# State-space stage of a ViT layer: three table products handed to GpSimd, weight loads begun by ScalarE, a third store buffer, a last chunk with summed operands

## The reference

```python
P = dt_Lambda[..., None] * pos - P_max[..., None]      # token h (128), state n (64), position l (1024)
Wc = Wc * num * _reciprocal(den * Lam, EPS)            # Wc: x as complex numbers
K = jnp.einsum('chn,hnl->chl', Wc, jnp.exp(P))         # c: 64 batch rows
return K.real
...
h = _L0_tok_ref(...)                                   # this stage: h0, 64 x 128 x 1024
h = h + _L0_attn_ref(_layernorm(h), Wq, Wk, Wv, Wo)    # second stage of the kernel, not touched
h = h + _L0_ffn_ref(_layernorm(h), A, B, Wr, br)       # second stage, not touched
```

## Time and profile before

| | us |
|---|---|
| median of 3 runs (2502.73 to 2509.3) | 2504.96 |
| the profiled execution | 2504.22 |
| its span, first to last instruction | 2502.4 |
| first matmul of s4_stage | 42.06 |
| first instruction of layer_stage | 300.40 |

### The profile page before, as it was taken

The page is one execution under the profiler, slowest core; times in us unless marked ns, Lnnn a source line. Parts: engine busy times, 40 slices in busy tenths (PEclk is TensorE's granted clock), DMA queues, the critical chain, the costliest instruction groups (busy, mean ns, idle before and its releaser), DMA issues.

```text
span 2502.4 us, 58994 instructions
## 1 busy us (share of the span) xinstructions
PE 2349.1 (94%) x18752; PEld 1245.7 (50%) x18752; DVE 1952.3 (78%) x7939; ACT 1850.1 (74%) x6398; POOL 1629.6 (65%) x1508
## 2 busy tenths in 40 slices
PE   2888679999999999999999999999999999999986
PEld 2677534444455544454455454444555545444543
DVE  8888547888788778788787778788887778887864
ACT  5777547777777777777777777777777777777773
POOL 1233147777777777777777777777777777777772
PEclk9999889999999999999999999999999999999997
DMA  2777559999999999999999999999999999999984
GB/s 74 215 210 213 166 103 167 176 184 184 182 186 188 183 177 179 186 185 184 181 188 186 185 174 181 185 185 184 184 187 184 179 181 182 184 186 186 182 164 101
DMA packets 1199527, 443.66 MB, mean 177 GB/s; under 512 B 1149552, under 2 KB 1151856, under 8 KB 1199216
## 3 DMA queue, kind: packets, MB, share of 16 engines
q1 hardware_dynamic: 1199216, 439.89, 88.9%
HBM read 87.42 MB, written 67.11 MB: 62 GB/s over the span
## 4 chain that ended last, share of the span: by engine, by line
PE 69%; DVE 13%; issue 2%; ACT 2%; POOL 1%; DMA 1%; POOLq 0%; DVEq 0%; ACTq 0%
PE pb L817 8%; PE pb L819 7%; PE pb L818 7%; PE pa L817 6%; PE pa L818 6%; PE pa L819 6%; PE pv_ps L846 4%; PE pc L817 4%; PE pc L818 4%; PE pc L819 4%; PE s_ps L831 4%; DVE pr L1111 2%; DVE bn L1130 2%; DVE h L1221 2%; DVE nrm L1144 2%
## 5 line engine op out<-in xcount | busy, mean ns | idle before, releaser
L968 ACT ACTIVATE pr<-pr,smin 128x128 f32<-128x128 f32 x2048 | 792.8, 389 | 111.5 <-DVE smin L1111 111.3
L1325 POOL TENSOR_TENSOR p<-pr,p 128x512 f16<-128x512 f32 x512 | 600.8, 1174 | 254.1 <-ACT p L978 244.0
L1317 POOL TENSOR_TENSOR pr<-pr,rinv 128x512 f32<-128x512 f32 x512 | 529.7, 1040 | 268.2 <-DVE rinv L1119 268.2
L978 ACT ACTIVATE p<-pr 128x512 f16<-128x512 f32 x512 | 319.6, 624 | 238.5 <-POOL pr L1317 218.6
L1111 DVE CUSTOM_DVE_ANT_0 pr<-s_ps,cst 128x128 f32<-128x128 f32 x2048 | 470.3, 284 | 27.0 <-POOL p L1325 13.9
L968 ACT ACTIVATION_READ_ACCUMULATOR pr<-pr,smin 128x1 f32 x2048 | 383.6, 187 | 0.0
L576 PE MATMUL hps<-z,xw 128*128 128x256 f32 x896 | 214.5, 402 | 80.4 <-POOL xw L304 42.1
L576 PEld LDWEIGHTS hps<-z,xw 128*128 128x128 f32 x896 | 179.8, 203 | 114.7 <-issue 45.8
L831 PEld LDWEIGHTS s_ps<-kt,qt 128*128 128x128 f16 x2048 | 152.7, 98 | 145.3 <-DVE smin L1111 45.4
L1165 DVE TENSOR_TENSOR xs<-h_ln,xs 128x512 f16<-128x512 f32 x128 | 123.7, 968 | 125.1 <-ACT xs L1013 125.1
L817 PE MATMUL pa<-wkv_hi,xt 128*128 128x512 f16 x512 | 197.2, 385 | 25.0 <-DMA xt<-xs 25.0
(11 more groups left out here) (189 smaller groups left out, 5747.1 us busy)
## 6 DMA issues: line engine op xcount, KB each, us to landing
h<-hout SPq DMA_DIRECT2D x128, 256.0 KB, 3.3
h_ln<-h SPq DMA_DIRECT2D x64, 512.0 KB, 4.3
h_res<-h SPq DMA_DIRECT2D x64, 512.0 KB, 4.7
out<-h SPq DMA_DIRECT2D x64, 512.0 KB, 5.4
pt<-p SPq DMA_TRANSPOSE x512, 3.3
xa<-x SPq DMA_DIRECT2D x16, 256.0 KB, 4.7
xb<-x SPq DMA_DIRECT2D x32, 128.0 KB, 4.0
wst<-wq SPq DMA_DIRECT2D x8, 512.0 KB, 5.3
```

Source lines behind the costliest of these rows:

```text
L968: last = A.activation(p, p, ACT.Exp, bias=smin[g % 2][:, j:j + 1], scale=-1.0, accum_out=rsum[g % 2][:, j:j + 1])
L978: A.activation(p16[g % 2][:, 0:HG * P], pr[g % 2][:, :], ACT.Copy).then_inc(ph_done, 1)
L1317: nc.gpsimd.tensor_tensor(p3, p3, rinv[g % 2][:, :].unsqueeze(2).broadcast_to([P, HG, P]), ALU.mult).then_inc(p_norm, 1)
L1325: nc.gpsimd.tensor_tensor(p[:, HG * P:], pr[g % 2][:, :], p[:, 0:HG * P], ALU.subtract).then_inc(pl_done, 1)
```

## The change

- `across`, and three operations, become functions that take an engine: `first_angles` (old L392), `table_i` (old L413), `digits_m1` (old L421). For k = 0 DVE does them as before. For later chunks POOL does them, each behind one of its window additions; DVE waits for them on a new semaphore `tab_p`.
- `HR` goes from 2 to 3.
- All pairs of the last chunk are summed (8 instead of 2).
- Weight loads leave SP's program for ACT's. Piece n >= 2 is begun at the start of ACT's window `max(due(n) - 2, due(n - 2))`.
- `wo` is due in W2 instead of W1; `aw` and `bm` in W0 of the next chunk instead of W2.
- `weight_hi` comes at the end of ACT's window before the one it is due in (`wq`: was at the start of W0, now at the end of W0; `wo`: was at the start of W1, now at its end; `wkv`: the same place as before).
- DVE's `weight_lo` comes behind the table work of its window instead of ahead of it.

```diff
-HR = 2
+HR = 3
...
-        TV, TA = 13, 3
+        TV, TA, TP = 10, 3, 3
...
         def summed(g):
-            return g % 2 == 1 and g // 2 % PER_CHUNK in SUM_AT
+            return g // (TC // 2) == CHUNKS - 1 or g % 2 == 1 and g // 2 % PER_CHUNK in SUM_AT
...
-            PIECES += [(4 * k + 1, "wq", k, D, 1), (4 * k + 1, "wo", k, D, 1)]
+            PIECES += [(4 * k + 1, "wq", k, D, 1), (4 * k + 2, "wo", k, D, 1), (4 * k + 3, "wkv", k, 512, 2)]
             if k < 2:
-                PIECES.append((4 * k + 2, ("aw", "bm")[k], None, (KC * AW, D)[k], 1))
-            PIECES.append((4 * k + 3, "wkv", k, 512, 2))
+                PIECES.append((4 * k + 4, ("aw", "bm")[k], None, (KC * AW, D)[k], 1))
...
+        def first_angles(eng, k):
+            return eng.tensor_tensor(theta[:, :, :], across(zi, k, NPOS),
+                                     pos[:, :].unsqueeze(1).broadcast_to([P, TC, NPOS]), ALU.mult)
+        def table_i(eng, k):
+            return eng.tensor_tensor(tab[k % 2][:, :, 1, :], expo[:, k * TC:k * TC + TC, :], theta[:, :, :], ALU.mult)
+        def digits_m1(eng, k):
+            return eng.tensor_tensor(dm1[:, :, :].rearrange("p t (s n) -> p t s n", s=2), across(rr, k, 2, DIG),
+                                     tab[k % 2][:, :, :, 0:DIG], ALU.mult)
...
 # gpsimd
+                pool.wait_ge(pre_v, N_PRE)
                 for w in range(WINDOWS):
                     add(w)
+                    k, at = (w - 1) // PER_CHUNK, (w - 1) % PER_CHUNK
+                    if w >= 1 and k + 1 < CHUNKS:
+                        if at == 0:
+                            pool.wait_ge(tab_v, TV * k + 10)
+                            first_angles(nc.gpsimd, k + 1).then_inc(tab_p, 1)
+                        if at == 2:
+                            pool.wait_ge(tab_a, TA * (k + 1) + 2)
+                            pool.wait_ge(z_made, k * (TC // 2))
+                            table_i(nc.gpsimd, k + 1).then_inc(tab_p, 1)
+                        if at == 3:
+                            pool.wait_ge(tab_v, TV * (k + 1) + 7)
+                            pool.wait_ge(tab_p, TP * (k + 1) + 2)
+                            digits_m1(nc.gpsimd, k + 1).then_inc(tab_p, 1)
...
 # scalar
+                for n in range(2):
+                    load_weight(n)
                 for w in range(WINDOWS):
                     k = w // PER_CHUNK
                     if w % PER_CHUNK == 1 and k + 1 < CHUNKS:
                         sines(k + 1)
                     for n, piece in enumerate(PIECES):
-                        if w == (piece[0] - 1 if piece[1] == "wq" else piece[0]):
-                            weight_hi(n)
+                        if n >= 2 and w == max(piece[0] - 2, PIECES[n - 2][0]):
+                            load_weight(n)
                     for e in range(WIN):
                         if e < ON_ACT and w + LEAD < WINDOWS:
                             products(w + LEAD, e)
                         evict(WIN * w + e)
+                    for n, piece in enumerate(PIECES):
+                        if piece[0] == w + 1:
+                            weight_hi(n)
...
 # vector, angles(k)
-                    V.tensor_tensor(theta[:, :, :], across(zi, k, NPOS),
-                                    pos[:, :].unsqueeze(1).broadcast_to([P, TC, NPOS]), ALU.mult).then_inc(tab_v, 1)
+                    if k == 0:
+                        first_angles(V, k).then_inc(tab_p, 1)
+                    dve.wait_ge(tab_p, TP * k + 1)
...
 # vector, loop over windows
-                    if at in SUM_AT:
-                        sum_z(2 * w + 1)
-                    for n, piece in enumerate(PIECES):
-                        if piece[0] == w:
-                            weight_lo(n)
+                    for g in (2 * w, 2 * w + 1):
+                        if summed(g):
+                            sum_z(g)
                     if k + 1 < CHUNKS:
...
                             digits(k + 1)
+                    for n, piece in enumerate(PIECES):
+                        if piece[0] == w:
+                            weight_lo(n)
```

More of the change, by code:

```diff
@@ L123, in vit_layer @@
         layer_stage(nc, h0, out, W)
-V_F, V_X, V_E, V_T = 15, 16, 17, 26
+V_F, V_X, V_E, V_T, N_PRE = 15, 16, 17, 26, 49
 def s4_stage(nc, x, log_dt, lam, wq, wk, wv, wo, aw, bm, br, consts, h0, W):
@@ L211, in s4_stage @@
         tab_a = sem("tab_a")
+        tab_p = sem("tab_p")
         pr_done = sem("pr_done")
@@ L246, in weight, with across @@
             return t[:, :, :].rearrange("p k n -> p (k n)") if name.startswith("aw") else t[:, :]
+        def across(row, k, *shape):
+            a = row[:, k * TC:k * TC + TC].unsqueeze(2)
+            return a.broadcast_to([P, TC, shape[0]]) if len(shape) == 1 else \
+                a.unsqueeze(3).broadcast_to([P, TC, *shape])
+        def first_angles(eng, k):
[6 more added lines that the diff above has]
+                                     tab[k % 2][:, :, :, 0:DIG], ALU.mult)
         with nc.Block() as block:
@@ L259, in load_x @@
                         sp.dma_start(xb[slot][r * NS:r * NS + NS, :, :], x[1 - r, :, toks, :]).then_inc(x_in[slot], 16)
[L261 to L269, removed]
                 def store(g):
@@ L290, in _ @@
                     store(2 * w)
-                    while sent < len(PIECES) and PIECES[sent - 2][0] <= w:
-                        load_weight(sent)
-                        sent += 1
                     store(2 * w + 1)
                 for i in range(HR):
-                    sp.wait_ge(h_sent[i], 32 * (T // 2 // HR))
+                    sp.wait_ge(h_sent[i], 32 * len(range(i, T // 2, HR)))
             @block.gpsimd
@@ L314, in sines @@
                 def sines(k):
-                    act.wait_ge(tab_v, TV * k + 6)
+                    act.wait_ge(tab_v, TV * k + 5)
                     A.activation(half[:, :, :], theta[:, :, :], ACT.Sin, scale=0.5).then_inc(tab_a, 1)
@@ L339, in evict, with load_weight @@
                     A.activation(hout[g % HR][:, t % 2, :], hps[t % 4][:, :], ACT.Copy).then_inc(h_copied, 1)
+                def load_weight(n):
+                    _, name, k, width, _ = PIECES[n]
+                    if n >= 2:
+                        act.wait_ge(w_lo, n - 1)
+                    at = 0
+                    for src in SRC[name]:
+                        piece = src if k is None else src[k * P:k * P + P, :]
+                        act.dma_start(wst[n % 2][:, at:at + piece.shape[1]], piece).then_inc(w_in[n % 2], 16)
+                        at += piece.shape[1]
                 def weight_hi(n):
@@ L412, in tables, with digits @@
                     V.tensor_scalar(half[:, :, :], half[:, :, :], -2.0, 1.0, ALU.mult, ALU.add).then_inc(tab_v, 1)
-                    V.tensor_tensor(at[:, :, 1, :], expo[:, toks, :], theta[:, :, :], ALU.mult).then_inc(tab_v, 1)
-                    dve.wait_ge(tab_v, TV * k + 7)
[L415 to L423, removed]
+                    if k == 0:
+                        table_i(V, k).then_inc(tab_p, 1)
+                    dve.wait_ge(tab_v, TV * k + 6)
+                    V.tensor_tensor(tab[k % 2][:, :, 0, :], expo[:, k * TC:k * TC + TC, :], half[:, :, :],
+                                    ALU.mult).then_inc(tab_v, 1)
+                def digits(k):
+                    m1, m2 = (a[:, :, :].rearrange("p t (s n) -> p t s n", s=2) for a in (dm1, dm2))
+                    dve.wait_ge(tab_v, TV * k + 7)
+                    dve.wait_ge(tab_p, TP * k + 2)
+                    if k == 0:
+                        digits_m1(V, k).then_inc(tab_p, 1)
+                    V.tensor_tensor(m2, across(ss, k, 2, DIG), tab[k % 2][:, :, :, 0:DIG], ALU.mult).then_inc(tab_v, 1)
+                    dve.wait_ge(tab_v, TV * k + 8)
+                    dve.wait_ge(tab_p, TP * k + 3)
                     V.tensor_tensor(u4[k % 2][:, :, 0, :], m1[:, :, 0, :], m2[:, :, 1, :], ALU.add).then_inc(tab_v, 1)
@@ L449, in table_z @@
                     if at == 0:
-                        dve.wait_ge(tab_v, TV * k + 13)
+                        dve.wait_ge(tab_v, TV * k + 10)
+                        dve.wait_ge(tab_p, TP * k + 2)
                     digit = u[k % 2][:, :].rearrange("p (s n) -> p s n", n=DIG)[:, 4 * at:4 * at + 4, :]
@@ L537, in _ @@
                 step(V.scalar_tensor_tensor(rr[:, :], gr, re_row, t0, ALU.mult, ALU.subtract))
+                assert steps[0] == N_PRE
                 tables(0)
@@ L544, in _ @@
                         swapped(w + 1)
-                    table_z(2 * w)
-                    table_z(2 * w + 1)
+                    for g in (2 * w, 2 * w + 1):
+                        table_z(g)
                     if w == 0:
                         swapped(1)
-                    if at in SUM_AT:
-                        sum_z(2 * w + 1)
-                    for n, piece in enumerate(PIECES):
-                        if piece[0] == w:
-                            weight_lo(n)
```

(3 more changed lines are left out.)

17 lines of the change are left out of this document (4 added, 13 removed).

## The result

| | before | changed |
|---|---|---|
| median, us (lowest to highest) | 2506.36 (2502.73 to 2509.3) | 2492.39 (2490.95 to 2493.57) |
| ratio to before, 95% interval | | 0.9945 (0.9927 to 0.9962) |
| profiled execution | 2504.22 | 2493.57 |
| first instruction of layer_stage (end of the first stage) | 300.40 | 288.29 |
| from there to the end of the span | 2202.0 | 2203.5 |

The change is 14 us faster (0.55%). In the two profiled executions, 10.7 us apart, the first stage is 12.1 us shorter and the rest 1.5 us longer. A later run of the same kernel gave 2490.99 and a first stage to 287.80. The median before is now that of four runs; the prediction had three of them (2504.96).

What follows compares the result with a forecast made beforehand. First stage bound by a ring of waits, not one engine. Chunks 3 to 6 -1.3, chunks 0 to 2 -3.5, last chunk -3.9: -8.7 us from 2504.22 gives 2495.5, median 0.7 higher, so 2496; range 2483 to 2506.

Steps and rivals of the forecast that it cites:

- the walk through one chunk: First stage, middle chunks: steps timed from W0's z pair; next chunk at 30.05 or, with PE slowed, 30.95 us, mean 30.7.
- the ring: First stage: PE, DVE and ACT wait on each other in a circle, so a PE gap returns half a chunk later.
- ACT's issue: ACT's program: beginning a weight load costs ACT 0.67 us for one, 1.6 us for wk and wv together.
- The clock: PE in W0, chunks 3 to 6: after a 2.3 us gap it runs mostly slowed, 30.7 us a chunk as mean.
- Now DVE sets it: Last chunk: with all pairs summed, DVE's instructions rather than PE set its length, 22.4 us against 26.3, -3.9 us.
- Third store buffer: ACT's evictions: waits for stores, 29.8 us in all, should go; store waits then costed at zero.
- Exclusion: POOL's operations and DVE's two-SBUF-input or fast one-input ones run one after the other; W3's pair, sum and digits take 5.5 us.
- Rival 2: POOL's products don't exclude DVE's; W3 is 1.1 us shorter in seven chunks, -7.7 us, so 2488; chance 0.1.
- eight early loads: Chunks 0 to 2, ACT: eight weight loads wait for a low part DVE makes at the end of that very window.
- Rival 1: Beginning a DMA costs ACT nothing: 12.2 us less on the critical waits, 2483.5; chance 0.2.
- Rival 3: ACT's beginning of loads is dear: at 2.25 us each about 2519, slower than before; chance 0.12.
- Rival 4: No change: stores hold the last chunk, its -3.9 us is lost, and POOL takes 1.34 us: 2501.5; chance 0.13.

Runs made afterwards that it cites:

- e1: Changed kernel with the last chunk summed only in the two pairs summed before: median 2497.74 us, first stage to 285.65.
- e11: e8 with weight_hi behind the second eviction of its window instead of the fourth: median 2468.83 us, first stage to 261.42.
- e8: Changed kernel with weight loads back in SP's program and the three products back on DVE: median 2472.42 us, first stage to 267.79.
- e7: Kernel before the change with three store buffers (HR = 3) and nothing else: median 2488.49 us, ratio 0.9939 to before.
- e2: Changed kernel with first_angles, table_i and digits_m1 done by DVE in every chunk: median 2487.95 us, first stage to 280.65.
- e3: Changed kernel with weight loads back in SP's program, between a window's two stores: median 2479.08 us, first stage to 276.22.
- e9: Changed kernel with ACT's weight loads begun behind the second eviction of the same window: median 2479.54 us, first stage to 276.15.
- e12: e11 with weight loads begun by ACT, behind the second eviction: median 2470.27 us, first stage to 264.21.
- e10: e8 with the last chunk summed only in the two pairs summed before: median 2473.02 us, first stage to 268.12.
- e6: Changed kernel with weight_lo ahead of its window's table work again: median 2492.29 us, first stage to 289.30.

## Why the prediction was right, and where it was not

The forecast of 2496 with a range of 2483 to 2506 held, in good part by luck: two terms were too small by 8.4 us together and one had the wrong sign, by 5.1. No part was priced by itself, so it isn't in the prediction that the third buffer alone gives 17 us, nor that the place of the loads and POOL's products cost 12.1 and 7.6 us of stage. Still, the walk through one chunk described the ring well: for chunk 4 it gave W1 to W3 and the next chunk at 8.1, 13.8 / 14.4, 22.45 / 23.35 and 30.05 / 30.95 us; the trace has 7.81, 14.37, 22.43 and 29.81. Of its signs, ACT's waits for stores and DVE's for theta and wo_hi came as it said; chunks 1 and 2 (32.3 and 32.2), the middle ones (29.6), ACT's loads and the last chunk did not.

- **Chunks 0 to 2: -7.6 us, forecast -3.5; chunks 3 to 6: -5.6, forecast -1.3.** The step that was mis-sized is ACT's issue. I took 0.67 and 1.6 us from SP's rows; ACT's cost 0.44 and 0.94. The 16 issues that I counted on the ring make 5 us of the 8.4. The rest is not accounted for one by one (first_angles took 1.05 instead of 1.2 us). The clock was sized right: of chunks 3 to 6 three were slowed in W0 (14.01 us for 56 records at 138.36, 168.16 and 226.99), and one not (7.14 for 32 at 197.96), all four after a gap of 1.95 to 1.96.
- **Last chunk: +1.2, forecast -3.9.** The failed step is "Now DVE sets it": I added up DVE's instructions and gave wq_lo no wait. The time line of ACT and DVE in the last chunk says otherwise:

```profile
265.55 0.60 ACT L354 ACTIVATE hout<-hps 128x512 f32<-128x512 f32 x1 [0.60 <-PE hps L607]
266.04 1.05 ACT L369 ACTIVATE wq_hi<-wst 128x1024 f16<-128x1024 f32 x1
...
267.12 1.23 DVE L494 SCALAR_TENSOR_TENSOR wq_lo<-wst,wq_hi 128x1024 f16<-128x1024 f32 x1 [2.80 <-ACT wq_hi L369]
```
  PE starts W0 later, since it waits for the sums (4.02 us idle), and then runs slowed (10.11 us for 32 records, plain 7.14); evictions, wq_hi, wq_lo and the next z tiles follow it. The sum also gave PE the full clock, and it had the half one for a good part of the chunk. The ring that I had walked for the middle chunks also held in the last one. e1 shows the sums' price (1.2 us); e11 shows that the place of the high parts counts, 3.0 us against e8 with nothing else changed, though it moves all of them and not wq_hi alone.
- **Third store buffer.** That the waits go was right. I priced it inside the walk and never alone, so the prediction does not say that this one number is worth as much as the whole change (e7: 17 us, the change 14). Beside it the remaining edits together gave nothing: the stage ends at 288.29 and 287.80 with them, at 286.39 without.
- **Products on POOL.** Exclusion was right in kind: W3's pair, sum and digits took 5.3 us (forecast 5.5), the tables 4.55 (4.65). The Trainium skill's page SBUF — State Buffer, section Who interferes with whom, says that a DVE instruction with two SBUF inputs contends with a GpSimd instruction that reads SBUF, and that the loser is blocked for the whole instruction; the trace agrees, L440 and L449 end 0.55 us after POOL's product. I did not draw the consequence that the move is a loss: 7.6 us of stage (e2), some of it by way of the clock. Rival 2 is out.
- **Loads on ACT.** I saw eight early loads that would wait and walked them (33.7 us for chunk 1; measured 32.3), but took them as a detail of a move that helped. The trace has four waits, 9.9 us together. e3 and e9 show that the loads at this place cost 12 us of stage, with the issues and the clock's share. The Trainium skill's page DMA: Bandwidth & Descriptors, section Issuing engines are not separate DMA queues, said that a second issuer saves only issue time; e12 against e11 agrees, since its own queue saved nothing even when well placed.
- **Rival 1** (a free issue) is out as it stands: 0.44 and 0.94 us are nearer to my 0.67 and 1.6 than to nothing, and so is the time. Behind the second eviction, though, the issues cost nothing that e9 against e3 could show (e12 against e11: 2.8 us of stage, and why was not looked for). **Rival 3** is out: no load cost ACT over 0.72 us to begin. **Rival 4** had the right outcome for the last chunk and the wrong cause: ACT did not wait for stores.
- **Not seen:** ACT's products wait 15.3 us for x, which SP begins behind the stores. This was not tried by itself. In e12 they wait longer (18.9 us) and the stage is 24 us shorter, so the sum of these waits is no measure of what they cost.
- What gave the gain that e8 has over e7 (18.6 us of stage, 14.9 of it in chunks 0 to 2) are the new due times and the places of the high parts, by elimination: the sums (e10) and the order of the low parts (e6) are near nothing, each tried beside one other kernel only. In e7 DVE still waits 5.7 us for aw_hi and 5.6 for bm_hi. Neither of the two was undone alone, so this part is argued and not shown.

## What to carry to other kernels

Price each edit alone as well as inside the new schedule: here one changed constant, a third buffer, gave at least as much as the whole change, and two of the other parts took away 20 us of stage that the rest had won (e8). When an instruction that waits is moved to another engine's program, ask what is queued behind it there and whether what it waits for can have happened by then: half a window later the same loads cost no more than from SP (e9 against e3). When a two-input elementwise product moves from DVE to POOL, look at what DVE does beside it: here its products with two SBUF inputs were held up (1.64 and 1.53 us instead of 0.68), and in the earlier trace rows a one-input tensor_scalar too, while the z tiles, with one input in PSUM, kept their 2.34 us a pair beside POOL's addition. And read the granted clock before a difference of 1 or 2 us is put down to an edit.

## What was not expected of the hardware

- Beginning the same weight load took ACT 0.33 us (wk) and 0.47 (wv) as the median of eight, and SP 0.67 and 0.93.
- The second stage, with the same code, took 2199.1 to 2207.9 us in the traces of the thirteen kernels, and repeated to 0.3 us in the one that was traced twice. That is as much as some of the edits are worth. Whether the first stage ahead of it decides it is not shown, and its cause is open.
- The same W0, after the same gap of 1.95 us, ran slowed in three of four chunks of one trace and two of four of another of the same kernel. With every pair of the last chunk summed, 32 of PE's records mostly took 8.6 to 10.2 us instead of 7.14, so that 43% fewer records bought little or nothing.
